# Deformable convolution and an RBF attention block on one core: tap products in quads of rows, product tiles stored from ACT's queue, sums, last table and x1 loads in other places

## The reference, cut to what matters

```
# layer 0
out    = relu(bn(conv1x1(x, w1)))                      # 1024 -> 256 channels
offset = conv3x3(out, w_off) + b_off                   # 18 numbers per pixel
out    = relu(bn(deform_conv3x3(out, offset, w2)))     # 9 taps, bilinear, 256 -> 256
x      = relu(bn(conv1x1(out, w3)) + x)                # 256 -> 1024, residual: "x1"
# layer 1
t, p, g = Wt x, Wp x, Wg x                             # three 1024 -> 512 products
att_k   = sum over the image of alpha_k p^k g          # k = 0, 1, 2
y       = sum_k att_k alpha_k t^k
z       = Wz y                                         # 512 -> 1024
out     = (z - mean) * rsqrt(var + eps) * gn_w + gn_b + x
```

## Time and profile before

| what | value |
|---|---|
| median of three runs | 2483.91 us (2478.66 to 2488.22) |
| the profiled execution's own time | 2480.86 us |
| its span, first to last instruction | 2478.7 us |
| mean granted TensorE clock | 0.962 |
| TensorE (PE) busy | 2303.1 us, 93% of the span |
| DVE, ACT, POOL busy | 1556.3, 1244.0, 768.9 us |
| DMA | 683.63 MB, mean 276 GB/s |

### The profile page before, as it was taken

One profiled execution on the slowest core, in us unless ns is written; L12 is line 12 of the kernel. 1 busy time (PEld: TensorE's weight loads), 2 busy tenths in 40 slices (PEclk: granted clock), 3 DMA queues, 4 the chain that ended last, 5 costly groups with the idle time before them and its releaser, 6 DMA issues.

```text
span 2478.7 us, 29477 instructions
## 1 busy us (share of the span) xinstructions
PE 2303.1 (93%) x10316; PEld 1892.4 (76%) x10316; DVE 1556.3 (63%) x3110; ACT 1244.0 (50%) x2432; POOL 768.9 (31%) x710
## 2 busy tenths in 40 slices
PE   7999999888996999999999999999999999998960
PEld 6888887777885878888878888888778878886850
DVE  4213126546527889888888888888794234456764
ACT  5444443333344566655555565655553324455664
POOL 0100003332402456554565667666560000000000
PEclk9999999889998999999999999999999999999985
DMA  8999999999996899898998989999884111117679
GB/s 281 298 283 277 294 275 341 344 333 363 336 337 236 299 339 351 312 330 312 333 315 290 338 313 335 329 315 334 293 318 150 56 64 51 51 48 266 220 280 392
DMA packets 321676, 683.63 MB, mean 276 GB/s; under 512 B 22296, under 2 KB 162456, under 8 KB 315384
## 3 DMA queue, kind: packets, MB, share of 16 engines
q1 hardware_dynamic: 215048, 300.80, 37.3%
q0 software_dynamic: 88048, 322.22, 36.8%
q10 hardware_dynamic: 18432, 58.73, 6.0%
HBM read 443.38 MB, written 238.29 MB: 275 GB/s over the span
## 4 chain that ended last, share of the span: by engine, by line
PE 78%; DMA 10%; DVE 5%; issue 2%; ACT 1%; POOL 1%; SPq 1%; another core or an unknown queue 0%; ACTq 0%; DVEq 0%; POOLq 0%
PE bank L138 21%; PE bank L140 21%; PE bank L139 21%; DMA vone<-vb 4%; PE bank L1292 4%; PE bank L1294 4%; PE bank L1293 4%; DMA g<-vwide,tbl 1%; DMA xt<-x 1%; PE bank L1316 1%; DVE z L1238 1%; DMA xb<-x 1%; DMA vwide<-vb 1%; SPq L375 1%; DVE a L921 1%
## 5 line engine op out<-in xcount | busy, mean ns | idle before, releaser
L567 POOL DMA_INDIRECT g<-vwide,tbl x512 | 584.3, 1141 | 696.0 <-DVE a L905 303.8
L138 PE MATMUL bank<-x1h,wlh 128*128 128x512 f32 x1536 | 605.3, 394 | 4.0 <-DVE x1l L1129 3.0
L140 PE MATMUL bank<-x1h,wll 128*128 128x512 f32 x1536 | 602.4, 392 | 2.9 <-issue 2.8
L139 PE MATMUL bank<-x1l,wlh 128*128 128x512 f32 x1536 | 601.8, 392 | 2.1 <-issue 2.0
L921 DVE SCALAR_TENSOR_TENSOR a<-g,tbl,a 128x256 f32<-128x256 f32 x1224 | 526.2, 476 | 41.7 <-DMA g<-vwide,tbl 37.2
L594 ACT ACTIVATE g<-g,tbl 128x256 f32<-128x256 f32 x1008 | 426.4, 498 | 242.7 <-DMA g<-vwide,tbl 135.5
L140 PEld LDWEIGHTS bank<-x1h,wll 128*128 128x128 f32 x1536 | 289.8, 189 | 69.4 <-issue 7.3
L138 PEld LDWEIGHTS bank<-x1h,wlh 128*128 128x128 f32 x1536 | 290.2, 189 | 66.9 <-issue 6.2
L139 PEld LDWEIGHTS bank<-x1l,wlh 128*128 128x128 f32 x1536 | 290.2, 189 | 62.4 <-issue 0.9
L647 ACT ACTIVATE vb<-bank 128x512 f32<-128x512 f32 (+1 forms) x320 | 167.4, 557 | 268.9 <-DMA vone<-vb 122.6
L1292 PE MATMUL bank<-w2h,o1h 128*128 128x512 f32 (+1 forms) x640 | 243.8, 381 | 32.3 <-ACT vb L647 32.3
(11 more groups left out here) (145 smaller groups left out, 3193.9 us busy)
## 6 DMA issues: line engine op xcount, KB each, us to landing
vwide<-vb SPq DMA_DIRECT2D x64, 1152.0 KB
vwide<-vb SPq DMA_DIRECT2D x64, 896.0 KB
xin<-in_x SPq DMA_DIRECT2D x64, 512.0 KB
xf<-in_x SPq DMA_DIRECT2D x32, 1024.0 KB
x<-xf ACTq DMA_DIRECT2D x32, 1024.0 KB, 5.9
out<-z SPq DMA_DIRECT2D x128, 256.0 KB, 4.6
xb<-x SPq DMA_DIRECT2D x38, 512.0 KB, 4.8
t<-ts ACTq DMA_DIRECT2D x64, 256.0 KB
```

Of the source, the lines that this page charges most:

```text
L138: nc.tensor.matmul(out, wh, xh, start=first, stop=False)
L139: nc.tensor.matmul(out, wh, xl, start=False, stop=False)
L140: return nc.tensor.matmul(out, wl, xh, start=False, stop=last)
L567: pool.indirect_dma_start(slot[:].rearrange("p a c -> p (a c)"), None, d["vwide"][img], bass.IndirectOffsetOnAxis(ap=at[:, i, tap(u), 0:1] ...
```

## The change

1. **Quads of rows.** A chunk's image rows are laid out in `O1H` and `O1L` by kind: odd ones first, then even ones. A tap product of 128 pixels now covers two rows of one kind, and the two kinds (a = 0, 1) of one group of two taps follow each other. `VB` becomes six buffers of two taps by two kinds (4 KB a partition). A pixel and the one below it then lie side by side in SBUF, and both halves of a wide row go out in one piece of 2 KB for half of the pixels; the other half still goes in two pieces of 1 KB. The DRAM tables have even and odd rows apart, and the row number in `tables` takes 12 instructions more (two kinds of taps: 35 in all; image 0, 27 in all).
2. **Stores from ACT's queue.** `store_v` moves from SP to ACT and is called by `v_evict` after each group of two taps: 15 stores for a quad (two tiles) in image 0, 16 in image 1, so 496 in all where SP issued 160. ACT waits for its own evictions (`v_ev`) ahead of each first store.
3. `O1H` and `O1L` have two buffers in place of three; `offsets(s - 2)` goes from the middle of step s to its start, in two halves of 256 columns, 24 matmuls in place of 12.
4. **Places.** Three units more in step 17 (39 in the first stretch), three fewer in chunk 0 of the second. `tables(3)` comes ahead of the second stretch and is stored by ACT at q = 2. The splits of weights 8 and 9 move to q = 1 and 2, of 10 to 12 to q = 4, of 13 to q = 6. `load_acl(2)` and `(3)` come ahead of the weights that they stood behind.
5. **x1.** In the z pass of image 0 the load of x1 goes ahead of the store; `adds_by` starts with one addition a tile; `XT` has 20 buffers, and six of the new loads are issued before the last matmul.

```diff
 def f_points():
-            if s == 9 and point > 2 or 10 <= s < 15 and point or s == 15 and point in (1, 3):
+            if s == 9 and point > 2 or 10 <= s < 15 and point or s == 15 and point in (1, 3) or s == 17 and point in (1, 3, 5):
...
 def p_points(start):
-            n = min(UNITS, first + 2 * TAPS * (q + 1) // GROUPS)
+            n = min(UNITS, first + (2 * TAPS if c else 2 * TAPS - 3) * (q + 1) // GROUPS)
...
 def adds_by(x):
-    return max(0, min(64, 3 * (x - 3) // 2, x + 4))
+    return max(0, min(64, max(x - 3, 3 * (x - 5) // 2), x + 4))
...
-    XT = XB + [... for i, at in enumerate([R1] * 4 + [G_AT] * 4 + [R2] * 4)]
+    early = [z_at[57], z_at[59], z_at[61], A_AT, A_AT + 4 * KB, R5 + 32 * KB]
+    XT = XB + [... for i, at in enumerate(early + [at + 4 * KB * i for at in (R1, G_AT, R2) for i in range(4)])]
...
+            def store_v(s, t, j):
+                quad = 2 * s + t // 2
+                img, y = quad // QUADS, 4 * (quad % QUADS)
+                g = 5 * quad + j
+                vb, done = VB[g % NVB], vb_out[img][g % NVB]
+                wide, one = group_taps(img, j)
+                act.wait_ge(v_ev, 10 * quad + 2 * j + 2)
+                def rows(table, at, taps):
+                    return table[at:at + taps * GRID].rearrange("(t r) c -> r t c", r=GRID)[y // 2 * SIDE:y // 2 * SIDE + 128]
+                if wide:
+                    table, at = d["vwide"][img], HEAD + 2 * j * GRID
+                    act.dma_start(rows(table, at + wide_even(WIDE[img]), wide), vb[:, 0:wide].rearrange("p t a c -> p t (a c)")).then_inc(done, 16)
+                    act.dma_start(rows(table, at + SIDE, wide)[:, :, 0:CMID], vb[:, 0:wide, 1, :]).then_inc(done, 16)
+                    act.dma_start(rows(table, at, wide)[:, :, CMID:2 * CMID], vb[:, 0:wide, 0, :]).then_inc(done, 16)
+                if one:
+                    at = HEAD + (2 * j + wide - WIDE[img]) * GRID
+                    for a in range(2):
+                        act.dma_start(rows(d["vone"][img], at + a * one_odd(WIDE[img]), one), vb[:, wide:wide + one, a, :]).then_inc(done, 16)
...
             def v_evict(s, t):
+                quad = 2 * s + t // 2
+                for j in PARTS[t % 2]:
+                    g, n = 5 * quad + j, min(2, TAPS - 2 * j)
+                    if g >= NVB:
+                        vb_wait(act, g - NVB)
+                    for a in range(2):
+                        count = 2 * g + a
+                        act.wait_ge(v_done, count + 1)
+                        nc.scalar.activation(VB[g % NVB][:, 0:n, a, :], RING[count % 4][:, 0:n * CMID].rearrange("p (t c) -> p t c", c=CMID), ACT.Copy).then_inc(v_ev, 1)
+                    store_v(s, t, j)
...
             for i in range(ZT):
-                store_out(i)
                 if i % 2:
                     load_x1(i // 2 + len(XB))
+                store_out(i)
...
-            for w in range(4, 10):
+            for w in range(4, 8):
                 split_low(w)
+            tables(3)
```

More of the change, by code:

```diff
@@ L303, in program, with group_taps, group_stores, vb_wait @@
     out_v = d["out"].rearrange("i (k p) n -> i p k n", p=128)
[L306 to L311, removed]
+    def group_taps(img, j):
+        n = min(2, TAPS - 2 * j)
+        wide = max(0, min(n, WIDE[img] - 2 * j))
+        return wide, n - wide
+    def group_stores(g):
+        wide, one = group_taps(g // (5 * QUADS), g % 5)
+        return (3 if wide else 0) + (2 if one else 0)
+    def vb_wait(eng, g):
+        img = g // (5 * QUADS)
+        eng.wait_ge(vb_out[img][g % NVB], 16 * sum(group_stores(i) for i in range(5 * QUADS * img, g + 1) if i % NVB == g % NVB))
+    def vb_all(eng, img):
+        for g in range(5 * QUADS * (img + 1) - NVB, 5 * QUADS * (img + 1)):
+            vb_wait(eng, g)
     def halo_h_count(s):
@@ L461, in load_acl @@
                 sp.dma_start(ACL[:], d["acc"][p]).then_inc(acl_in, 16)
-            for w in range(7, 12):
+            load_acl(2)
+            for w in range(7, 11):
+                stage(w)
+            load_acl(3)
+            for w in range(11, 13):
                 stage(w)
@@ L595, in gather, with f_gather, table @@
                 ins.then_inc(prod_done, 1)
+            def f_gather(s, point):
+                i = 7 * s + point
+                for u in range(F_ENDS[i - 1] if i else 0, F_ENDS[i]):
+                    if shared(u // TAPS):
+                        gather(u)
+            def table():
+                act.wait_ge(tab_done, 4)
+                act.dma_start(d["tbl"][1][:, HALF:2 * HALF], TAB[:]).then_inc(tab_last, 16)
             def store_sums(k):
@@ new lines, in tables, with index @@
+                link(nc.vector.tensor_copy(place, whole))
+                link(nc.vector.tensor_tensor(over, place, half, ALU.subtract))
+                link(nc.vector.tensor_scalar(over, over, 0.0, None, ALU.is_gt))
+                link(nc.vector.tensor_tensor(place, place, over, ALU.subtract))
+                def index(column, taps, by_place, by_row, more):
+                    at, row, col = ix[:, :, taps], fy[:, :, taps], fx[:, :, taps]
+                    link(nc.vector.scalar_tensor_tensor(out=at, in0=place[:, :, taps], scalar=float(by_place), in1=BASEI[:, img, :, taps], op0=ALU.mult, op1=ALU.add))
+                    link(nc.vector.scalar_tensor_tensor(out=at, in0=row, scalar=float(by_row), in1=at, op0=ALU.mult, op1=ALU.add))
+                    link(nc.vector.scalar_tensor_tensor(out=at, in0=col, scalar=float(more), in1=at, op0=ALU.add, op1=ALU.add))
+                    return nc.vector.tensor_copy(ints[:, :, taps, column], at)
@@ L1303, in offsets @@
                 at_least(pe, y_done, s)
-                for i in range(6):
-                    k, dy = i // 3, i % 3
-                    rows = slice(dy, dy + ROWS)
-                    nc.tensor.matmul(YP[0:OFFM, :], WOA[:, i, :], O1H[r][:, k, rows, :], start=i == 0, stop=False)
-                    last = nc.tensor.matmul(YP[0:OFFM, :], WOB[:, i, :], O1L[r][:, k, rows, :], start=False, stop=i == 5)
+                for b in range(2):
+                    out = YP[0:OFFM, :].rearrange("p (m b x) -> p b m x", b=2, x=SIDE)[:, b]
+                    for i in range(6):
+                        at = i // 3 * O1_ROWS * SIDE + row_at(i % 3 + b)
+                        for part, w in ((O1H, WOA), (O1L, WOB)):
+                            last = nc.tensor.matmul(out, w[:, i, :], part[r][:, at:at + 4 * SIDE].rearrange("p (m x) -> p m x", x=SIDE),
+                                                    start=i == 0 and w is WOA, stop=i == 5 and w is WOB)
                 last.then_inc(yp_done, 1)
```

244 lines of the change are left out of this document (134 added, 110 removed).

## The result

| | before | after |
|---|---|---|
| median of seven runs | 2478.66 us (2464.34 to 2488.22) | 2499.82 us (2493.11 to 2504.29) |
| profiled execution, its span | 2480.86, 2478.7 us | 2503.20, 2501.4 us |

The change makes the kernel slower by 0.8%: ratio 1.008, 95% interval 1.0052 to 1.0107. The forecast was 2450 in a range of 2422 to 2484; the time fell outside, on the side of the first rival. A second series (e11) gave 1.0088 (1.0057 to 1.0119), so the sign and size hold.

A forecast was written before the change was run, and what follows sets the result against it. PE was taken to bound image 0 and DMA, through the stores, image 1. Terms -12 + 2.4 - 5 - 11 - 8 = -33.6 from 2480.86 gave 2447.3, with the median 3.05 above: 2450, range 2422 to 2484 us.

The forecast's parts named there:

- first rival: Slower: ACT, which empties PSUM, is held by its own store issues; 5 us a chunk, 2502 us in all; chance 0.12.
- one ACT issue of 128 partitions takes 0.33 us: Image 0: 30 new ACT issues a chunk cost 10 to 11 us, covered by PE's 41.03 us.
- a term of 0: Image 0's chunks: DMA demand falls 4.8 us a chunk, but PE is the bound there, so 0.
- Image 1: Six chunks bound by DMA through the stores; 2 KB pieces move faster: -12 us, at best -50.7.
- third rival: Image 1 nearly reaches PE's pace, as SP's blocked issues held back x: chunks 43 to 45 us, 2425; chance 0.12.
- Offsets in halves: 24 matmuls of 256 columns in place of 12 of 512: 0.15 us for 16 chunks, +2.4 us.
- The transition: Into the second stretch: PE's restart hangs on DVE and comes at 800 for 805.06, -5 us; bounds -20 and +6.
- The z pass: Load of x1 ahead of the store goes out 6 to 8 us earlier, removing DVE's wait: -11 us.
- The tail: Behind the last matmul: six of 12 loads of 512 KB leave, 3.1 MB at 391 GB/s, -8 us.
- Table length: Twelve more instructions of `tables` are hidden in images 0 and 1, where DVE has 28 of 50 us: no cost.

The follow-up runs named there:

- e11: The changed kernel, unedited, run and profiled again: ratio 1.0088 to the kernel before; profiled execution 2499.74 us.
- e1: The changed kernel with every product store issued by SyncE (SP) instead of ACT, same stores and shapes: ratio 0.979 to the kernel before.
- e5: As e1, but the store of 2 KB pieces is split in two of 1 KB pieces: ratio 0.9805 to the kernel before.
- e9: e1 with 36 units in the first stretch, additions up to eight tiles ahead, and tables(0) to tables(2) ahead of point 5's units: 2415.12 us, ratio 0.9747.
- e8: e1 with 36 units in the first stretch and 18 in the second's first chunk, as before the change: ratio 0.9747 to the kernel before.
- e4: The kernel before with only the change's x1 order of loads and additions, XT keeping 14 buffers: ratio 0.9987 to the kernel before.
- e2: The changed kernel with only the third store of a wide group issued by SyncE (SP), the rest by ACT: ratio 0.9876 to the kernel before.
- e3: The kernel before, its few large product stores issued by ACT behind the tile's last eviction: ratio 1.0162 to the kernel before.
- e12: The kernel before, unedited, run and profiled again: ratio 1.000; profiled execution 2476.14 us.

## Why the prediction was wrong

**The step that failed** is the sentence that "one ACT issue of 128 partitions takes 0.33 us" and the 10 to 11 us that followed for 30 issues. The row was of single stores that stand alone, of 256 KB. Three in a row took 0.37, 0.53 and 0.90, 1.80 us a group and 18 to 20 us a chunk, where the sum had 10 to 11. I also weighed ACT by its sum over the chunk (18.4 + 11 of 41 us), where the products are made in bursts against a ring of four banks: the test that decides is one group of ACT against one of PE, 3.07 against 2.73. That comparison was open to me; with 1.1 us of issues it would have read 2.3, so the size of the term made the error, and the sum over the chunk hid how thin the margin was. The start and image 0 came out at +36.6 us for a term of 0. With this one step undone (e1) the ratio is 0.979, some 50 us faster, where my sum had 33.6.

**The first rival had the mechanism's place but another form.** It asked for over 11 us of ACT's time a chunk, which 18 us of issues meet, and gave 2502 us. Its evidence was SP's long holds in full stretches; in image 0 the DMA share was 0.73 and nothing was held up by full engines. Its sign, issues over 1 us in the median, did not show either (0.37, 0.53, 0.89): it had 5 us a chunk right without the reason. It also added a loss in image 1, which did not come.

**Image 1** shows the -12 that I forecast in one pair of profiles and -2.7 in the other, and either is luck, the rest of two errors: finer stores are worth 22 to 36 us with SP issuing, and ACT's issues take some 25 back. The pieces of 2 KB, my reason, are worth 5 us at most (e5). The third rival's chunks of 43 to 45 us came true once the stores left ACT (269.3 us for six, 44.9). Its reason did not: in e1 SyncE issues x and all stores in one queue, as before.

**Offsets in halves:** +2.4 forecast for sixteen chunks; 41.10 us for 41.03 in e1, about 1.

**The transition:** -5 forecast. The change has +15.4 - 9.3 = +6.1 in the ledger and +9.0 in the first two profiles, at and past the upper bound of +6; with the stores on SP (e1) 209.6 for 215.5 and 213.8 us in the two profiles of before, -4 to -6. The units moved to step 17 cost 4 to 7 (e9, e8).

**The z pass:** -11 forecast, -5.7 measured, and 7 in e4. The gap near 2250 went, but one of 4.79 us stands at 2299, again before DVE's `yl`. **The tail:** -8 forecast, -1.0 measured. I read the order of the loads in SP's program and not the wait ahead of them.

**Table length:** costed at nothing beside DVE's 28 of 50 us. In chunk 13 the 12.7 us meet a late gather and PE stands for 11 to 12 us. Again a share of a chunk was taken as cover. How much of this is the 12 new instructions and how much the late gather is open.

## What to carry to other kernels

Count DMA issues as work of the engine that makes them, at the length they have when several follow each other, and weigh one unit of its loop against one unit of the engine that it feeds; a busy share leaves the issues out and averages over bursts. Where an engine waits for buffers, try stores small enough that buffers come free one at a time, and let an engine issue them on which nothing waits. When a transfer is moved to be early, look at the wait that stands ahead of it in that queue.

## What the runs showed of the hardware

- Issue lengths on ACT: 0.33 us alone (before), 0.37, 0.53 and 0.90 in a row in image 0. With one of the three moved to SP and ahead of the others (e2) it took 0.36 and ACT's second 1.07: the sum stayed at 1.80. All three on SP (e1, 100 to 360 us) took 0.71, 0.68 and 1.16 in the median, with the DMA engines at 0.85 instead of 0.73.
- An issue of ACT took 0.33 us while one of SP stood for 6.89 us around it (before, 533.93 us).
- Issues of 1,152 pieces took 0.51 us in the median in image 0 and up to 3.7; in image 1 the third one of a tile, of 256 pieces to `vone`, took 3.1 in the median and up to 14.2 (e3).
- Pieces of 1 KB moved at 313 GB/s beside x in the kernel before and at 352 in e5, so the size of the piece alone does not set the price.
- In one execution of the kernel before two chunks of the second stretch took 82.6 and 85.9 us for 76.6, with PE idle for 3.1 and 3.2 us and a mean granted clock of 0.98 and 0.96; in another (e12) no chunk did.
